# A recurrent layer whose state is the initial matrix plus a growing sum of outer products

## The reference

```python
outputs = einsum('bci,boi->bco', chunk, M)            # M: 128 x 128 per batch
k_mean  = mean over the chunk of chunk / |chunk|
v_target = mean(silu(outputs @ vg_w1.T) @ vg_w2.T + outputs)
err  = v_target - M @ k_mean
M_new = alpha * M + eta * outer(err, k_mean)
M_new = gate * M_new + (1 - gate) * M
scale = minimum(30 / (norm(M_new) + 1e-6), 1)
M = M_new * scale
final_out = value_gen(all outputs)                    # silu(y @ vg_w1.T) @ vg_w2.T + y
```

## Time and profile before

| | |
|---|---|
| median of 3 runs | 1222.33 us (1217.41 to 1224.69) |
| the profiled execution: time, span | 1221.05 us, 1219.0 us |
| TensorE busy | 1085.7 us (89%) |
| VectorE busy | 886.4 us (73%) |
| ScalarE busy | 836.6 us (69%) |
| GpSimd busy | 228.2 us (19%) |
| granted TensorE clock, mean | 0.911 |

### The profile page before, as it was taken

How to read it: one execution, slowest core, us unless ns; L and a number is a source line. 1 busy time by engine, 2 the same in 40 slices (tenths; PEclk the granted TensorE clock), 3 DMA queues, 4 the chain that set the end, 5 groups by cost and what they waited for, 6 DMA issues and landing times.

```text
span 1219.0 us, 21224 instructions
## 1 busy us (share of the span) xinstructions
PE 1085.7 (89%) x5149; PEld 693.6 (57%) x5181; DVE 886.4 (73%) x2120; ACT 836.6 (69%) x1285; POOL 228.2 (19%) x328
## 2 busy tenths in 40 slices
PE   5629999999997679999999999999978998399997
PEld 2202222322223457777777777777757877378776
DVE  6863434344344859999999999999986787869997
ACT  5439999999995458888888888888851322156665
POOL 7453544445442100000000000000022111100000
PEclk9769999999999889999999999999985566589999
DMA  3464666666664066666666666666510000032331
GB/s 94 116 177 155 214 203 205 219 197 216 207 196 142 22 246 219 244 226 223 239 226 223 244 221 231 241 216 236 194 52 1 0 0 0 0 119 95 112 108 35
DMA packets 92908, 192.47 MB, mean 158 GB/s; under 512 B 9672, under 2 KB 56392, under 8 KB 82632
## 3 DMA queue, kind: packets, MB, share of 16 engines
q1 hardware_dynamic: 92880, 192.15, 46.3%
HBM read 154.03 MB, written 38.08 MB: 158 GB/s over the span
## 4 chain that ended last, share of the span: by engine, by line
PE 80%; DVE 9%; issue 3%; ACT 3%; DMA 1%; POOL 1%; ACTq 0%; DVEq 0%; SPq 0%; POOLq 0%
PE bank L1150 24%; PE bank L1163 14%; PE bank L1020 9%; PE bank L1157 8%; PE bank L1002 6%; PE bank L1005 5%; PE bank L1244 2%; PE bank L1237 2%; ACT ring L803 2%; PE bank L1031 1%; PE bank L1232 1%; PE bank L1241 1%; DMA ring<-c_rows 1%; PE bank L928 1%; DVE xn L1332 1%
## 5 line engine op out<-in xcount | busy, mean ns | idle before, releaser
L803 ACT ACTIVATE ring<-bank,minus_bound 128x1024 f32<-128x1024 f32 x256 | 271.3, 1111 | 30.7 <-PE bank L1005 13.6
L1150 PE MATMUL bank<-xh,w_parts 128*128 128x512 f32 x896 | 279.8, 393 | 1.9 <-issue 1.9
L1545 DVE TENSOR_TENSOR hl<-q_stack,hh 128x512 fp32r<-128x512 f32 x386 | 264.4, 685 | 0.2
L1555 DVE TENSOR_TENSOR q_stack<-q_stack,ring 128x512 f32<-128x512 f32 x320 | 221.6, 693 | 51.4 <-DMA ring<-c_rows 10.7
L853 ACT ACTIVATE hh<-q_stack 128x512 fp32r<-128x512 f32 x386 | 243.3, 630 | 19.3 <-DVE q_stack L1721 14.2
L860 ACT ACTIVATE q_stack<-bank 128x512 f32<-128x512 f32 x320 | 191.8, 600 | 87.3 <-PE bank L1150 87.3
L1163 PE MATMUL bank<-hh,w_parts 128*128 128x512 f32 x776 | 242.7, 394 | 0.0
L1415 DVE TENSOR_TENSOR bank<-bank,corner 128x128 f32<-128x128 f32 x256 | 76.6, 299 | 173.7 <-PE bank L1005 145.1
L1150 PEld LDWEIGHTS bank<-xh,w_parts 128*128 128x128 f32 x896 | 169.0, 189 | 40.7 <-issue 2.3
L1150 PE MATMUL bank<-xl,w_parts 128*128 128x512 f32 x448 | 176.4, 394 | 0.0
L1157 PE MATMUL bank<-hl,w_parts 128*128 128x512 f32 x390 | 167.1, 428 | 5.8 <-DVE hl L1545 5.8
(11 more groups left out here) (258 smaller groups left out, 1173.1 us busy)
## 6 DMA issues: line engine op xcount, KB each, us to landing
ring<-c_rows SPq DMA_DIRECT2D x80, 1024.0 KB, 5.1
w_parts<-w_pairs SPq DMA_DIRECT2D x160, 128.0 KB, 2.7
w_pairs<-xh SPq DMA_DIRECT2D x16, 768.0 KB, 4.4
q_stack<-q_parts SPq DMA_DIRECT2D x64, 144.0 KB
k_stack<-k_parts SPq DMA_DIRECT2D x64, 144.0 KB
w_pairs<-xl SPq DMA_DIRECT2D x16, 512.0 KB, 3.5
ring<-c_rows SPq DMA_DIRECT2D x16, 512.0 KB, 4.5
big<-in_w_exp SPq DMA_DIRECT2D x16, 384.0 KB, 4.8
```

The lines of the kernel that those rows point to most:

```text
L803: act.activation(ring[:, c % RING * S:(c % RING + 1) * S], wide[c % 2][:], ACT.Exp, bias=minus_bound[:]).then_inc(exp_done, 1)
L1150: ins = pe.matmul(out_, w[i], x_[j], start=start and k == 0, stop=stop and k == 2, skip_group_check=not start)
L1545: dve.tensor_tensor(hl[(c - 1) % 2][:], hid[(c - 1) % 2], hh[(c - 1) % 2][:].bitcast(F32), ALU.subtract).then_inc(split, 1)
L1555: dve.tensor_tensor(hid[c % 2], act_out[c % 2], cb[u][:, g * GW:(g + 1) * GW], ALU.mult).then_inc(hid_ready, 1)
```

## The change

The state M is no longer kept. After n steps it is c times (M0 + sum over j of e_j k_j^T), with one scalar c and one column e_j per step. So:

- Ahead of the chain TensorE multiplies all tokens once with the initial state times vg_w1 (`base_z`, into banks 0 to 3, left open for accumulation), all tokens with all key means (`kx`), and makes the pairwise products of the keys by a matmul with ones over `k_pairs`; VectorE masks `kx` and scales these tables.
- In a step a matmul with 16 rows adds the past outer products to the chunk's z; the silu's sum goes through vg2T as a single column (q); VectorE forms the new column e, its part of the squared norm, and the offsets for the next step; two matmuls turn the columns e into rows (once times vg1T, once times the identity), which ScalarE copies to `e_rows`; a matmul with ones sums the norm's part, GpSimd takes the root per batch, VectorE makes the clip factor c per batch.
- The outputs are made in every second step for 128 tokens at a time, by three matmuls per batch, and are added to x at once; the turning back after the chain is gone.
- The hardware loops of this layer are written out. Semaphores of the attention's slow branch now share those of its fast one.

The diff, cut and moved left by twelve blanks; removed loop bodies are those described above.

```diff
@@ block.gpsimd @@
-link(pool.memset(m_norm[:], 0.0))
+link.sign(pool.memset(k_pad[:], 0.0))
+link.sign(pool.memset(e_cols[:], 0.0))
+link.sign(pool.memset(c_tok[:], 1.0))
+link.sign(pool.memset(c_all[:], 1.0))
+link(pool.memset(before[:], 1.0))
+link(pool.affine_select(out=before[:], in_=before[:], compare_op=ALU.is_ge, fill=0.0, base=-1,
+                        pattern=[[32, 2], [1, NCH]], channel_multiplier=-1))
+link(pool.tensor_copy(before[32:64, 0, :], before[32:64, 1, :]))
...
-pool.wait_ge(steps_ready, 1)
+pool.wait_ge(chain_open, 1)
+for n in range(NCH - 1):
+    for b in range(B):
+        pool.wait_ge(nu_ready[b], n + 1)
+        pool.tensor_tensor(m_len[:, b:b + 1], nu[:, b:b + 1], root[:, 0:1], ALU.pow).then_inc(len_ready[b], 1)
+    at = 64 * ((n + 1) % 2)
+    for b in range(B):
+        c_next = c_all[:, b, n + 1:n + 2]
+        pool.wait_ge(c_ready[b], n + 1)
+        link(pool.tensor_tensor(ac[:, b:b + 1], c_next, a_coef[:, b, n + 1:n + 2], ALU.mult))
+        link(pool.tensor_copy(c_tok[at:at + 64, b * QT + (n + 1) // 2:b * QT + (n + 1) // 2 + 1], c_all[at:at + 64, b, n + 1:n + 2]))
+        pool.tensor_scalar(ac30[:, b:b + 1], ac[:, b:b + 1], MAX_NORM, None, ALU.mult).then_inc(ac_ready[b], 1)
@@ block.scalar @@
...
 act.wait_ge(fold_psum, 1)
+act.activation(m0vg1[:], bank(2)[:, 0:D], ACT.Copy).then_inc(fold_ready, 1)
...
+act.wait_ge(chain_open, 1)
+for n in range(NCH):
+    for b in range(B):
+        at = b * S + n * CH
+        act.wait_ge(z_done[b], n + 1)
+        if n:
+            act.wait_ge(c_ready[b], n)
+        act.activation(silu_z[:, at:at + CH], bank(at // 512)[:, at % 512:at % 512 + CH], ACT.Silu,
+                       scale=c_all[:, b, n:n + 1], accum_out=h_sum[:, b:b + 1]).then_inc(silu_done[b], 1)
+    if n < NCH - 1:
         for b in range(B):
-            ready(act, mz_psum[b], n)
-            act.activation(silu_z[b][:], bank(b)[:, 0:CH], ACT.Silu, scale=m_norm[:, 3, b:b + 1],
-                           accum_out=h_sum[b][:]).then_inc(mz_silu[b], 1)
-        for b in range(B):
-            ready(act, out_taken[b], n)
-            act.activation(memT[:, bass.ds(i * (2 * CH) + (b * S + u * CH), CH)], out_sum[b][:],
-                           ACT.Copy).then_inc(out_copied[b], 1)
+            act.wait_ge(e_psum[b], n + 1)
+            act.activation(e_rows[n % 2][32 * b:32 * b + NCH, :], bank(4 + b)[32 * b:32 * b + NCH, 0:2 * D], ACT.Copy)\
+                .then_inc(rows_ready[b], 1)
@@ block.tensor @@
...
+pe.matmul(bank(2)[:, 0:D], m0[:], vg1T[:], start=True, stop=True)
+pe.matmul(bank(2)[:, D:D + 1], ones[:], m0_rows[:], start=True, stop=True).then_inc(fold_psum, 1)
...
+pe.wait_ge(fold_ready, 1)
+pe.wait_ge(km_ready, 2)
+def base_z(b):
+    for h in range(2):
+        at = b * S + h * 512
+        pe.matmul(bank(2 * b + h), m0vg1[:], xnT[:, at:at + 512], start=True, stop=False, skip_group_check=True)
+for h in range(2):
+    for b in range(B):
+        ins = pe.matmul(bank(6 + h)[32 * b:32 * b + 32, :], k_pad[:, b, :], xnT[:, b * S + h * 512:b * S + (h + 1) * 512],
+                        start=True, stop=True, skip_group_check=True)
+    ins.then_inc(kx_psum, 1)
+pe.wait_ge(km_ready, 5)
+pe.matmul(bank(4), ones[:], k_pairs[:, 0, :], start=True, stop=True).then_inc(links_psum, 1)
+base_z(0)
+pe.wait_ge(tok_ready, 3)
+pe.matmul(bank(5)[:, 0:4 * NCH], m0T[:], dk[:, :, :, :].rearrange("p k b n -> p (k b n)"), start=True, stop=True)\
+    .then_inc(dk_psum, 1)
+base_z(1)
+pe.wait_ge(kx_ready, 1)
+pe.matmul(bank(6), ones[:], k_pairs[:, 1, :], start=True, stop=True).then_inc(links_psum, 1)
+pe.wait_ge(chain_open, 1)
+for n in range(NCH):
+    for b in range(B):
+        at, low = b * S + n * CH, 32 * b
+        z = bank(at // 512)[:, at % 512:at % 512 + CH]
+        if n:
+            pe.wait_ge(rows_ready[b], n)
+            pe.matmul(z, e_rows[(n - 1) % 2][low:low + NCH, 0:D], kx[low:low + NCH, n * CH:(n + 1) * CH], start=False, stop=True,
+                      skip_group_check=True).then_inc(z_done[b], 1)
+        else:
+            pe.sem_inc(z_done[b], 1)
+    for b in range(B):
+        pe.wait_ge(silu_done[b], n + 1)
+        if n < NCH - 1:
+            pe.matmul(bank(4 + b)[:, 2 * D:2 * D + 1], vg2T[:], h_sum[:, b:b + 1], start=True, stop=True).then_inc(q_done[b], 1)
+    if n < NCH - 1:
         for b in range(B):
+            low = 32 * b
+            pe.wait_ge(e_ready[b], n + 1)
+            pe.matmul(bank(4 + b)[low:low + NCH, 0:D], e_cols[:, b, :], vg1T[:], start=True, stop=True)
+            pe.matmul(bank(4 + b)[low:low + NCH, D:2 * D], e_cols[:, b, :], ident[:], start=True, stop=True).then_inc(e_psum[b], 1)
         for b in range(B):
+            pe.wait_ge(pr_ready[b], n + 1)
+            pe.matmul(bank(6 + b)[:, 2 * D:2 * D + 1], ones[:], e_pr[:, b:b + 1], start=True, stop=True)\
+                .then_inc(dot_psum[b], 1)
+    if n % 2:
         for b in range(B):
+            tile, low = b * QT + n // 2, 32 * b
+            tokens = slice(tile * P, (tile + 1) * P)
+            pe.wait_ge(nu_ready[b], min(n + 1, NCH - 1))
+            pe.matmul(bank(6 + b)[:, 0:D], xnT[:, tokens], m0T[:], start=True, stop=False)
+            pe.matmul(bank(6 + b)[:, 0:D], kx[low:low + NCH, n // 2 * P:(n // 2 + 1) * P], e_rows[(n - 1) % 2][low:low + NCH, D:2 * D],
+                      start=False, stop=True)
+            pe.matmul(bank(6 + b)[:, D:2 * D], silu_z[:, tokens], vg2T[:], start=True, stop=True).then_inc(out_psum[b], 1)
@@ block.vector @@
...
+dve.tensor_copy(dk[:, 1, :, :], by_batch(bank(4)[:, 0:C2])).then_inc(km_ready, 1)
 dve.wait_ge(km_ready, 1)
+dve.tensor_copy(k_pad[:, :, 0:NCH], dk[:, 1, :, :]).then_inc(km_ready, 1)
+dve.scalar_tensor_tensor(dk[:, 0, :, :], by_batch(x_mean[:]), 1.0 / CH, dk[:, 1, :, :], ALU.mult, ALU.subtract).then_inc(km_ready, 1)
+dve.wait_ge(km_ready, 3)
+for k in range(2):
+    dve.tensor_tensor(k_pairs[:, k, :].rearrange("p (b n j) -> p b n j", b=B, n=NCH), pairs(dk[:, 1, :, :], False),
+                      pairs(dk[:, k, :, :], True), ALU.mult).then_inc(km_ready, 1)
+dve.wait_ge(tok_ready, 3)
+link.sign(dve.tensor_scalar(a_coef[:], by_batch(rows[3]), -1.0, 1.0, ALU.mult, ALU.add))
+link(dve.reciprocal(rho[:], a_coef[:]))
+link(dve.tensor_tensor(rho[:], rho[:], by_batch(rows[1]), ALU.mult))
+link.sign(dve.tensor_scalar(rho64[:], rho[:], 1.0 / CH, None, ALU.mult))
+for h in range(2):
+    dve.wait_ge(kx_psum, h + 1)
+    mask = before[:, 0, 8 * h:8 * h + 8]
+    dve.tensor_tensor(kx[:, h * 512:(h + 1) * 512].rearrange("p (n t) -> p n t", t=CH),
+                      bank(6 + h)[0:64, :].rearrange("p (n t) -> p n t", t=CH),
+                      bass.AP(mask.tensor, mask.offset, [list(mask.ap[0]), [1, 8], [0, CH]]), ALU.mult).then_inc(kx_ready, 1)
+dve.wait_ge(dk_psum, 1)
+link.sign(dve.tensor_tensor(off0[:], m0_dk[:, 0, :, :], rho[:], ALU.mult))
+link.sign(dve.tensor_scalar(y0[:], m0_dk[:, 1, :, :], 2.0, None, ALU.mult))
+link.sign(dve.tensor_tensor(links_l, bank(4).rearrange("p (b n j) -> p b n j", b=B, n=NCH), pairs(rho[:], True), ALU.mult))
+dve.wait_ge(links_psum, 2)
+link.wait()
+link(dve.tensor_scalar(links_k, bank(6).rearrange("p (b n j) -> p b n j", b=B, n=NCH), 2.0, None, ALU.mult))
+link.sign(dve.tensor_scalar(kappa[:], diag, 0.5, None, ALU.mult))
+link.sign(dve.tensor_copy(off[:], off0[:, :, 0]))
...
+dve.sem_inc(chain_open, 1)
+for n in range(NCH):
+    for b in range(B if n < NCH - 1 else 0):
+        col = slice(b, b + 1)
+        dve.wait_ge(q_done[b], n + 1)
+        link.wait()
+        dve.scalar_tensor_tensor(e_cols[:, b, n:n + 1], bank(4 + b)[:, 2 * D:2 * D + 1], gamma[:, col], off[:, col],
+                                 ALU.mult, ALU.add).then_inc(e_ready[b], 1)
+        dve.wait_ge(e_ready[b], n + 1)
+        link(dve.scalar_tensor_tensor(e_w[:, col], e_cols[:, b, n:n + 1], kappa[:, b, n:n + 1], y2[:, col], ALU.mult, ALU.add))
+        dve.tensor_tensor(e_pr[:, col], e_cols[:, b, n:n + 1], e_w[:, col], ALU.mult).then_inc(pr_ready[b], 1)
+    for b in range(B if n < NCH - 1 else 0):
+        col = slice(b, b + 1)
+        link.sign(dve.tensor_tensor_reduce(junk[:, 0, b, :], e_cols[:, b, :], links_l[:, b, n + 1, :], 1.0, off0[:, b, n + 1:n + 2],
+                                      ALU.mult, ALU.add, off[:, col]))
+        link.sign(dve.tensor_tensor_reduce(junk[:, 1, b, :], e_cols[:, b, :], links_k[:, b, n + 1, :], 1.0, y0[:, b, n + 1:n + 2],
+                                           ALU.mult, ALU.add, y2[:, col]))
+    for b in range(B if n < NCH - 1 else 0):
+        col = slice(b, b + 1)
+        dve.wait_ge(dot_psum[b], n + 1)
+        dve.tensor_scalar(nu[:, col], bank(6 + b)[:, 2 * D:2 * D + 1], nu[:, col], 0.0, ALU.add, ALU.max)\
+            .then_inc(nu_ready[b], 1)
+    for b in range(B if n < NCH - 1 else 0):
+        col = slice(b, b + 1)
+        dve.wait_ge(len_ready[b], n + 1)
+        if n:
+            dve.wait_ge(ac_ready[b], n)
```

(74 more changed lines are left out.)

177 lines of the change are left out of this document (49 added, 128 removed).

## The result

| | before | after |
|---|---|---|
| median, 7 runs each on the same chip | 1220.83 us (1217.41 to 1224.69) | 1230.94 us (1228.97 to 1232.61) |
| span of the profiled execution | 1219.0 us | 1230.5 us |
| TensorE, VectorE busy | 1085.7, 886.4 us | 1094.2, 875.7 us |
| ScalarE, GpSimd busy | 836.6, 228.2 us | 830.8, 248.5 us |
| granted TensorE clock, mean | 0.911 | 0.904 |

The ratio after to before is 1.0086 [1.0065, 1.0106]: slower by about 10 us. The forecast was + 5.7, from the first median of 1222.33 to 1228, in a range of 1209 to 1240; it had the right sign and about half the size. The profiled executions are 0.2 above their median before (1221.05) and 1.4 above it after (1232.3), so their difference is 11.2 us in time, and 11.5 in span, where the medians give 10.1.

A forecast was written before the change was run, and what follows sets the result against it. TensorE's matmuls at 1.2 GHz were taken to bound the chain, 6.63 us a step. First silu 941.0 + chain 97.5 + 4.9 behind = 1043.4 against 1037.98; with 0.7 at the start + 6.1, so 1228 us, range 1209 to 1240.

The forecast's parts named there:

- The new step, even: Recurrent chain, steps without output matmuls: 5.4 us from one silu of batch 0 to the next, eight such periods.
- The new step, odd: Recurrent chain, steps with outputs of 128 tokens in TensorE's program before the next z: 7.75 us, seven such periods.
- Six matmuls of 128 columns, 2.76: Output matmuls of an odd step on TensorE, at 0.46 us each: 2.76 us together.
- The lag of batch 1: Batch 1's clip factor comes about 0.6 us after batch 0's out of the even step, moving q by 0.3.
- Ahead of the chain: Ten wide fp32 matmuls for tables, scaling and table load before the chain: first silu at 941.0, 7.7 us later.
- After the chain: From the last silu: batch 1's lag, six output matmuls, drain and last additions, 4.9 us; transposes gone.
- At the start: GpSimd gets eight small instructions for one, 2.4 us against 1.73 idle: + 0.7 us, bounds 0 and 2.4.
- The clock comes back: Chain at 2.4 GHz: steps of 5.3 us, 18 us less, 1210 us; warm for half, 1219; chance 0.27.
- The tables cost more: Ten wide matmuls ahead of the chain stay at 1.2 GHz: 17.5 instead of 10.9 us, 1234.6; chance 0.08.
- More hops than I count: Crossings between engines in the new step cost 0.5 us a step more: + 7.5 us, 1235.5; chance 0.15.
- the open terms: Uncertain prices of 128-column matmuls, table load, start and power, giving 1221 to 1236 us for the forecast as summed.

The follow-up runs named there:

- the replaced product: Changed kernel with the second output matmul of each batch (16 rows, kx with e_rows) replaced by a repetition of xnT with m0T (128 rows): 1219.08 us, once.
- four dummies: Changed kernel plus four bf16 matmuls of 255 columns behind z in every step, read by nothing: 1231.75 us, once.
- with eight: Changed kernel with outputs spread over following steps and tables reordered, plus eight unread bf16 matmuls of 255 columns a step: 1207.46 us, once.
- the spread and reordered kernel: Changed kernel with output matmuls moved behind later steps' z, second pair sums ahead of base_z(1), opening wait moved to TensorE's first q: 1204.86 us, ratio 0.9854 to before.
- four a step: Changed kernel with outputs spread over following steps and tables reordered, plus four unread bf16 matmuls of 255 columns a step: 1212.99 us, once.

## Why the prediction was right in sign and half the size

**The new step, even.** 5.26 us against 5.4. From the silu's start to nu it took 3.54 instead of 3.80, as the four matmuls with e took 1.50 and not 1.76; the power took 0.58 instead of 0.62; from nu to the next silu 1.72 instead of 1.6. Right.

**The new step, odd: the step that failed.** 8.61 against 7.75. "Six matmuls of 128 columns, 2.76" measured 4.01 us in that step (L1302 at 992.18 to L1279 at 996.19). The lag of batch 1 is there, with 1.21 us from the first q to the matmuls with e, as I had it (0.91 + 0.3). But those four took 1.34 instead of 1.76, the norm's pair 0.94 instead of 0.86, and z with its hop 0.65 instead of 0.72. 7.75 + 1.25 - 0.42 + 0.08 - 0.07 = 8.6. Seven such steps and eight even ones make 102.4 us; I had 97.5. The mis-sized term is the price of a 16-row matmul among 128-row ones: I took 0.46, with 0.37 and 0.52 as bounds, from rows in which every loaded matrix has 128 rows, and the six took 0.67 each. I noted only for z that no row shows one of 16, and the second output product has one too. With rows of 128 throughout the six took 2.86 us, near my 2.76. The price lies not in the instruction but in its neighbours. I had asked only whether a load of few rows is itself cheaper. Another page of the Trainium skill than the one I cited, "TensorEngine Tiling (Array Packing)", section Key Properties, has the rule that bears: changing the tiling mode drains TensorE. The trace and the replaced product agree with it, at 0.30 us a change; that the 16-row product puts TensorE in another mode is my reading, as no view shows the mode.

**Ahead of the chain.** From k_mean's copy to the first silu I had 15.0 us (941.0 less the copy, itself 0.2 later than 925.76), and 13.84 were measured. The ten wide matmuls and the small one took 10.2 us (928.28 to 938.49) against 11.1. Two errors partly cancel: the clock rose at about 933.9, 5.6 us after the first of them and not 4; and the four for kx took 0.89 us each at 1.2 GHz, half the 1.75 of rows 5. From there to the silu it was 2.8 us instead of 3.3. The table load behind the opening was right, 1.28 us. That 941.32 lies so near 941.0 is luck: a copy that came 1.5 us late and a stretch behind it that was 1.2 us short cancel, and the six later kernels with this opening have their first silu at 938.3 to 940.5.

**After the chain.** 6.07 against 4.9: the same six matmuls and the same 1.2 us.

**At the start.** I gave 0.7 us for GpSimd's new instructions. Its first iota starts at 4.36 us instead of 3.55 in the two timelines, but before its first norm instruction GpSimd still waits 1.33 us for VectorE's first statistics, where it waited 1.73, so they were hidden. That first norm instruction still comes 0.4 us later, at 8.37 instead of 7.96, as VectorE's statistics do; in the later kernels it stands between 7.71 and 8.52. The + 1.7 us at k_mean's copy is not shown to be the change: kernels of this study with the same instructions up to there have the copy at 925.5, 926.3, 926.7, 927.4 and 927.9.

**The rivals.** *The clock comes back* did not happen: 0.50 from 950 on, at 87% busy here and at 99% with four dummies. *The tables cost more*: its condition came true and its price did not. The clock had not risen by the third wide matmul, only for the last five of the ten, but the four for kx cost half of what I gave them. *More hops than I count*: no, the even step is shorter than summed; what was too long is TensorE's own work in the odd one.

The sum of the errors is + 4.9 in the chain, + 1.2 behind it, - 1.2 ahead of it and + 1.5 in the time up to k_mean's copy: 6.4, and norm(3) begins at 1049.79 where I had 1043.4 (1044.1 with the 0.7 for the start). So one cause carries the miss, the changes of rows, with 8.8 us in seven odd steps and 1.2 behind them; smaller terms take 3.9 of the chain's part back.

Three small slips of the prediction change nothing: the 256-column products are 3.95 of 6.63 us, 60% and not two thirds; the terms behind the chain add up to 4.8; the low end of the open terms is 1222.

## What to carry to other kernels

Put matmuls whose loaded matrices have the same number of rows next to each other: the order of six alone was worth 11 us here. When a state of 256-column products is replaced by small ones, the bound moves from work to latency, and then the work that is left belongs into the wait that latency opens (here 5.5 us a step, against 5.3 without any output). Keep a wait on the engine that needs the data, not on one whose table load would run ahead of it; here that and the order of one matmul gave about 3 us together.

## What the runs showed of the hardware

- A change between a loaded matrix of 128 rows and one of 16 costs 0.30 us at 1.2 GHz (1.18 for four). Products of 16 rows in different groups of 32 rows, one for each batch, take 0.59 us as a pair at 128 columns.
- Four matmuls with 32 loaded columns each, 512 streamed, alternating between two groups of output partitions, took 3.56 us at 1.2 GHz; one with 128 loaded columns took 1.87 (931.84 to 933.71). A matmul of 16 loaded columns without such an alternation takes 1.75, so fewer columns alone do not explain it. By these starts I take it that the two groups run side by side. The Trainium skill ("TensorEngine Tiling (Array Packing)", Key Properties) states that different tiles can work in parallel; the rate agrees.
- The clock does not follow busy time. TensorE was busy for 99% over 20 us at 0.50, with fp32 matmuls and four dummies; with eight it stood between 0.68 and 1.00 at 85 to 97% busy. In the kernel with the 16-row output product replaced, a stretch of 5 us (965 to 970), busy for 3.5 of them, has 0.84 right behind an odd step with six outputs back to back, and the step from 965.71 took 4.42 us instead of 5.26. Over 950 to 1020 the spread and reordered kernel has 0.50 without dummies, 0.55 with four a step and 0.83 with eight. What exactly the clock follows stays open.
